# Who fetches the score maxima back from HBM, and where the fetch stands in the queue of large loads

## The reference, cut to what matters

```python
q = (Q @ WQ + bQ), k = (K @ WK + bK), v = (V @ WV + bV)      # 8 batches, 256 tokens, 16 heads of 16
scores = einsum('bhqd,bhkd->bhqk', q, k) * SCALE
scores = where(causal, scores, -inf)
probs = softmax(scores)
out = einsum('bhqk,bhkd->bhqd', probs, v)
x = x + out @ WO + bO                                        # then the router and the experts
```

## Time and profile before

| What | Value |
| --- | --- |
| median of 3 runs | 689.99 us (688.66 to 690.61) |
| the profiled execution | 694.89 us |
| its span, first to last instruction | 693.2 us |
| mean granted TensorE clock | 0.928 |
| PE, PEld, DVE, ACT, POOL busy | 607.4, 504.8, 496.9, 353.4, 334.9 us |
| stretch of the steps of groups 2 to 15 | about 252 to 376 us of the span |
| q1 (SyncE's queue): bytes, share of 16 engines' span | 72.85 MB, 37.5% |
| q10 (ScalarE's queue): bytes, share | 0.23 MB, 0.1% |

### The profile page before, as it was taken

The page is one execution under the profiler, slowest core; times in us unless marked ns, Lnnn a source line. Parts: engine busy times, 40 slices in busy tenths (PEclk is TensorE's granted clock), DMA queues, the critical chain, the costliest instruction groups (busy, mean ns, idle before and its releaser), DMA issues.

```text
span 693.2 us, 11918 instructions
## 1 busy us (share of the span) xinstructions
PE 607.4 (88%) x4100; PEld 504.8 (73%) x4100; DVE 496.9 (72%) x1066; ACT 353.4 (51%) x685; POOL 334.9 (48%) x322
## 2 busy tenths in 40 slices
PE   3788999999997788999998716999999999999992
PEld 2566887887885545465565416999999999999991
DVE  6887788787788767767883532787887888778740
ACT  4774654753634234353545213566666666656551
POOL 1065425234240014321444574446686868686676
PEclk9898999999999999898998656999999999999997
DMA  9311416765359647755745006233626262621224
GB/s 287 115 32 38 114 31 161 257 184 151 93 129 241 149 102 196 181 141 140 186 134 186 25 13 232 67 119 63 175 29 177 28 180 32 172 30 14 27 32 46
DMA packets 63316, 81.65 MB, mean 118 GB/s; under 512 B 10295, under 2 KB 47938, under 8 KB 63256
## 3 DMA queue, kind: packets, MB, share of 16 engines
q1 hardware_dynamic: 53928, 72.85, 37.5%
q0 software_dynamic: 9216, 7.81, 7.8%
q10 hardware_dynamic: 112, 0.23, 0.1%
HBM read 48.27 MB, written 34.36 MB: 119 GB/s over the span
## 4 chain that ended last, share of the span: by engine, by line
PE 44%; DVE 5%; POOL 4%; issue 4%; DMA 3%; ACT 3%; ACTq 0%; SPq 0%; DVEq 0%; POOLq 0%
PE l_scores L101 14%; PE l_turned L1901 7%; PE l_out L1901 3%; PE l_shared L1901 3%; PE l_turned L340 3%; PE l_out L360 2%; POOL out L1605 2%; PE l_turned L324 2%; PE l_scores L1835 2%; PE l_shared L1777 2%; DMA l_hi<-md 1%; ACT l_area L370 1%; PE l_scores L265 1%; PE l_scores L1858 1%; PE l_scores L280 1%
## 5 line engine op out<-in xcount | busy, mean ns | idle before, releaser
L2090 DVE SCALAR_TENSOR_TENSOR w_v<-w_th,l_scores 128x324 f32<-128x324 f32 x128 | 62.2, 490 | 55.6 <-ACT w_th L1692 55.2
L1692 ACT ACTIVATE w_th<-l_scores 128x324 f32<-128x324 f32 x128 | 56.5, 442 | 83.2 <-PE l_scores L101 82.4
L1592 POOL TENSOR_TENSOR l_lo<-w_v,l_hi 128x324 fp32r<-128x324 f32 x64 | 59.1, 923 | 74.2 <-ACT l_hi L1698 74.0
L370 ACT ACTIVATE l_area<-l_turned 128x1024 f32<-128x1024 f32 x48 | 49.2, 1025 | 86.7 <-PE l_turned L340 86.4
L101 PE MATMUL l_scores<-l_hi,w_w1h 128*128 128x324 f32 x256 | 81.0, 316 | 2.3 <-DVE l_lo L2082 1.2
L1605 POOL DMA_INDIRECT out<-l_area,w_to x48 | 76.4, 1591 | 12.0 <-issue 9.6
L101 PE MATMUL l_scores<-l_lo,w_w1h 128*128 128x324 f32 x256 | 80.4, 314 | 0.0
L101 PE MATMUL l_scores<-l_hi,w_w1l 128*128 128x324 f32 x256 | 80.2, 313 | 0.0
L294 DVE TENSOR_REDUCE l_nm<-l_scores 128x4 f32<-128x1024 f32 (+1 forms) x45 | 54.7, 1216 | 22.4 <-PE l_scores L280 22.3
L1698 ACT ACTIVATE l_hi<-w_v 128x324 fp32r<-128x324 f32 x128 | 59.9, 472 | 12.4 <-DVE w_v L2090 11.8
L2064 DVE TENSOR_TENSOR w_w2l<-w_s,w_w2h 128x256 fp32r<-128x256 f32 x56 | 60.2, 1075 | 1.9
(11 more groups left out here) (350 smaller groups left out, 1709.5 us busy)
## 6 DMA issues: line engine op xcount, KB each, us to landing
w_s<-in_L_ffn_w SPq DMA_DIRECT2D x14, 1024.0 KB, 6.7
disp<-c_blank SPq DMA_DIRECT2D x8, 658.1 KB
l_lo<-kd SPq DMA_DIRECT2D x26, 200.0 KB
l_hi<-qd SPq DMA_DIRECT2D x26, 192.0 KB
w_rows<-disp SPq DMA_DIRECT2D x7, 658.1 KB
kd<-l_qkh SPq DMA_DIRECT2D x16, 256.0 KB, 4.7
vd<-l_area SPq DMA_DIRECT2D x4, 1024.0 KB, 6.5
qd<-l_qkh SPq DMA_DIRECT2D x16, 256.0 KB, 4.7
```

The source lines that it names most:

```text
L370: act.activation(lead.pr[n % 3][:, :], lead.tbank[:, :], ACT.Exp, scale=SCALE).then_inc(A["exp"], 1)
L1592: pool.tensor_tensor(hl[:, g % 3, half(1)], v[:, n % 4, :], hh[:, g % 3, half(1)].bitcast(F32), ALU.subtract)\
L1692: act.activation(th[:, n % 2, :], hb[n % 2][:, 0:HALF], ACT.Tanh, scale=0.5).then_inc(F["th"], 1)
L2090: dve.scalar_tensor_tensor(v[:, n % 4, :], th[:, n % 2, :], 1.0, hb[n % 2][:, 0:HALF], ALU.add, ALU.mult).then_inc(F["v"], 1)
```

## The change

SyncE issues the fetch of group g right behind the store of group g, so it first waits for the store's landing, and everything else of that group stands behind the fetch. ScalarE's fetch is taken out. The second call of `queries` moves from group 5 to group 6.

```diff
@@ SyncE
                 for g in range(2, GR):
                     store_maxima(sp, A, lead, md, g)
+                    load_maxima(sp, A, lead, md, g)
                     if g % 2 == 0 and g >= 4:
                         load_values(sp, A, M, lead, vd, g // 2)
                     if 5 < g + 3 < GR:
@@
                     if g % 2 == 1:
                         first_weights(g // 2)
-                    if g in (4, 5):
-                        queries(g - 4)
+                    if g in (4, 6):
+                        queries(g // 2 - 2)
                     if g == GR - 1:
                         weights(1)
@@ ScalarE
                     if t < NS:
                         exps(act, A, lead, t)
-                    if t % 3 == 1 and 2 <= (t + 2) // 3 < GR:
-                        load_maxima(act, A, lead, md, (t + 2) // 3)
```

## The result

The changed kernel took 699.94 us (698.25 to 701.63, four runs) against 690.3 us (688.66 to 693.02) of the kernel before on the same chip: a ratio of 1.0105, 95% interval 1.0062 to 1.0148. It is slower, by about 7 us by the ratio. The two medians are 9.6 us apart (1.4%); the text goes by the ratios, which come with an interval. The profiled execution took 701.09 us (span 699.4) against 694.89 (span 693.2).

What follows compares the result with a forecast made beforehand. PE bounds the kernel, losing time to late fetches and slow clock; after the change SyncE's queue becomes the bound. Group 13's fetch comes 7.1 us later, so 690.0 goes to 697 us, range 685.5 to 703.5 (forecast's own 693 to 701).

Steps and rivals of the forecast that it cites:

- The queue's serial cycle: SyncE's queue, groups 3 to 12: loads, store's landing (0.5 us) and fetch issue (0.65) no longer overlap, about 10.2 us.
- SyncE's waits of over 2 us: Sign of being right: SyncE waits over 2 us for the landing of stores in most groups.
- the moments without packets: Sign of being right: stretches without packets between one group's loads and the next; no size given.
- The stalls of 2 to 4 us at groups 5, 7, 11 and 13: Sign of being right: PE stalls 2 to 4 us at these groups' first turned scores, and none at 4.
- Step by step: Groups 2 to 13: times of loads, stores, fetches and PE, ending with group 13's fetch at 364.8, 7.1 us behind.
- The quiet fetch: Fetch on SyncE's queue with nothing beside it: taken as 1.9 us, the store's own time; bounds 1 and 5.4.
- The size of the cycle: Queue time per group: 8.95 us odd, 9.75 even, 11.75 with queries, 11.25 with the residual; about 10.2 on average.
- The break-even of 9.4: Groups 4 to 12: a cycle averaging 9.4 us equals today's 357.67 at group 13; below that the change wins.
- what PE wants at full clock: Groups 3 to 12: PE's own periods without stalls, 7.1 to 10.6 us, on average 8.4.
- The operands of g + 3: Loads wanted nine steps after DVE gives the maxima, so a delay of some 3 to 8 us is hidden.
- The queue keeps up: Rival, groups 4 to 12: cycle below 9.4 us, so faster, 685.5 us likelier, 681.5 in full; chance 0.24.
- ScalarE: 14 pairs of issues of 0.54 us leave ScalarE; counted as 0, covered by its wait for PE's turned scores.

Runs made afterwards that it cites:

- The light pair: Kernel before and changed kernel, each without values of batches 2 to 7, queries in group 2, residual stores at the end: ratios 1.0096 and 1.0058.
- the run with the wait alone: Kernel before with SyncE's wait for each store's landing put behind that store, the fetch left on ScalarE: ratio 1.0068.
- the early fetches: Kernel before with ScalarE's fetch one step earlier from group 3 on, SyncE waiting for nothing new: ratio 1.0105.

## Why the prediction was right

**The direction and the mechanism.** The forecast was 697 us, 7.1 above the kernel before; measured were 699.9, and 7.2 more by the ratio. The queue's serial cycle is what the traces show: the store lands late behind the last group's loads, the fetch goes out then, the loads behind it. The light pair shows it as the cause of the longer stretch: take loads off the queue and 5.5 us become 0.4. Of the signs named, SyncE's waits of over 2 us hold (its stores landed 2.8 to 7.7 us after their issue in every group from 4 to 13), and so do the moments without packets (285 to 286 and 294 to 295 us at a DMA share of 0.00 and 0.02). The stalls of 2 to 4 us at groups 5, 7, 11 and 13 do not: 3.04, 1.09, 0.31 and 0.58.

**Step by step**, taken from the start of group 2 so that the 2.9 us ahead of it drop out (261.12 against 258.25 in the earlier trace rows). Group 4: forecast 274.2, measured 274.1, its stall gone. Group 5: forecast 285.0 with a stall of 3.7, measured 284.3 with 3.04. Group 6: 295.4, measured 295.6. Group 7: 305.7 with a stall of 3.1, measured 304.1 with 1.09. Group 13: 364.8, measured 361.8.

**The quiet fetch.** 1.9 us was taken; 1.88 was measured at group 5.

**The size of the cycle** was the term that was too large: 9.86 us instead of 10.2 on average. By group: 11.2 and 10.95 with the queries (11.75 forecast), 8.8 behind group 5 (8.95), and 12.2 instead of 11.25 for the last with the residual. The error of 2.8 us in nine cycles was the larger part of the 3.0 at group 13. The break-even of 9.4 was near: by the forecast's own reckoning about half a microsecond per group decided the sign.

**What the sum left out.** The stretch grew by 4.1 us in the first pair and 5.5 in the mean of two. The forecast had 7.1 there, all as lateness of the queue; in the traces 2.1 of 5.5 are standing and 3.4 are longer work at a lower mean clock. The term behind this is what PE wants at full clock: the forecast gave it 51.7 us from group 7 to 13, far less than the queue's 59.1. Measured were 57.7 us, of which PE stood for the fetch for only 0.9, while the fetches of groups 7 and 13 went out 57.8 us apart. So queue and PE kept nearly the same pace there; the queue was not the clear bound that the sum made of it. The remainder of the measured 7 to 9.6 us lies in stretches that the change does not touch, and it differs between profiles of one kernel. So the nearness of 697 to 699.9 is partly luck.

**Readings that were wrong, without weight for the sum.** Group 7 was put in at 10.6 us, where the earlier trace rows give 10.9. The operands of g + 3 are wanted seven steps after DVE gives the maxima, not nine (3g - 4 and 3g + 3 by the loop); PE stood for none of them in either profile. And the fetch of 5.39 us overtook nothing to speak of: the store of queries issued behind it, at 270.21, landed 5.4 us later, at 275.6, the fetch at 275.4.

**The rivals.** "The queue keeps up" fails at the named place: stores landed 4 us after issue in groups 4 to 7, not 2. The rule of the Trainium skill (DMA: Bandwidth & Descriptors, section Issuing engines are not separate DMA queues), that issuing from another engine only saves issue time, holds for the DMA engines; it does not cover a wait, which holds back what stands behind it on the issuing engine. The light pair agrees with the rule where nothing is late (0.4 us). The same page's rule on turns between queues (section Queues, rings and completion order) no run here tests by itself. What the traces show is that a queue of its own did not spare the fetch the loads. From its second issue it needed 5.39, 5.46 and 4.72 us at groups 4, 6 and 10 of the kernel before and 4.58 at group 10 of the run with the wait alone, against 1.59 and 1.62 in the changed kernel.

**ScalarE** gained nothing, as counted: PE stood for its exponentials for 2.9 and 4.6 us before and 4.4 and 4.2 after.

## What to carry to other kernels

A fetch that must wait for its store's landing makes everything behind it on the issuing engine wait too; if the queue's loads already fill most of a period, as the 8 to 11 us of loads did here, stores that land 3 to 8 us after their issue are enough to make PE late. Work out the whole cycle (drain, landing, fetch, next loads) against the period of the bounding engine before moving such a wait, and look at what stands behind it, on a compute engine as well: there the early fetches cost 7 us, as much as the change. And before believing a stage's gain, look at the clock granted to it and at the stages behind it.

## What I had not expected of the hardware

In this stretch the granted clock moved more than the stalls themselves. The same program took 96.4 and 99.4 us at 0.96 and 0.91. Where two stalls of 1.3 us were taken away it ran through at 1.00 and needed 92.2, 4.3 to 7.3 us less for 2.6 us of stalls. These are three profiles, and the gain stayed in the stretch: the program's time did not follow.
